# A decoder layer's mixer with its heads ordered by lane group: one or two wide transfers for each factor and coefficient load, operands stored by batch, sums of squares in groups of four

## The chip, the cores and the metric

The kernel runs on one core of a Trainium2 chip. The metric is the device time of one execution in microseconds. Before the change three runs gave a median of 3355.25 us (3353.84 to 3386.32).

## The reference

A pre-norm decoder layer in float32 on x (4 batches, 1024 tokens, 256 channels): a state-space mixer, a cross-attention to 77 context rows, and a mixture of experts, each added to x. The change is in the mixer alone:

```python
bc = jnp.einsum('bti,oi->bto', value, W_bc).reshape(Bsz, Tlen, H, 4, N)
bc = bc / (jnp.sqrt(jnp.sum(bc * bc, axis=-1, keepdims=True)) + EPS)
Bz, Bx, Cz, Cx = (bc[..., 0, :], bc[..., 1, :], bc[..., 2, :], bc[..., 3, :])
def step(carry, inp):
    z, s = carry
    S = 1.0 / (1.0 + dt_t[..., None] * k_t[..., None] + (dt_t * dt_t)[..., None] * A)
    z = S[..., None] * (z - dtE * A[None, :, :, None] * s + dtE * (Bz_t[..., None] * u_t[:, :, None, :]))
    s = s + dtE * z + dtE * (Bx_t[..., None] * u_t[:, :, None, :])
    y = jnp.einsum('bhn,bhnd->bhd', Cz_t, z) + jnp.einsum('bhn,bhnd->bhd', Cx_t, s)
```

There are H = 32 heads of N = 32 states and 16 channels.

## The kernel before

`mixer` works in 16 units `u` of 64 time steps by 4 batches (256 columns, UT). The 32 heads stand in 8 groups `g` of 4 lane groups `j` (32 partitions each); two groups `g` make a pair, so a unit has four pairs `gp` (GP), and `n = 4u + gp` numbers them. Head `g*4 + j` lies in lane group `j`. In `bc`, `fb`, `fc`, `coef` and `pinv` a column is a time step and a batch, `t*4 + b`: the batch is innermost. Each engine has its own program, written out by hand, and they meet at semaphores; SP issues all transfers of the mixer in one program order.

PE: for a later pair, `projected` (four products of 128 x 512, line 605) and `summed` (line 619), which adds the squares of 32 states of a head with the 0/1 matrix `sel`, two of the four vectors at a time. For the pair in hand, `inputs_turned` (line 630), `causal_products` (643), `mixed_states` (663 and 673), `mixed_values` (683), once a unit `outputs` (692). The operands from `bc` are taken with `turns(...)[:, :, b]`, every fourth column.

ACT copies the projected tile to `bc` and squares it into `sq` (one buffer, lines 758 and 761), makes the inverse norms (`norms`), and scales the coefficients (`coefs`).

DVE: `evolve` is the recurrence of a 2 x 2 matrix over 64 steps (lines 918 and 924); `factors(n)` multiplies the inverse norms by step factors (944); `inputs(u,gp)` (957 to 971) and `read_out(u,gp)` (979 to 994) scale and mix the four vectors of a pair; `mask` (1002), `post` (1014 to 1024) and `residual` (1031) follow PE's results. Their order in a unit is in the last loop of DVE's program: `read_out` 0, `post` of the unit before, `inputs` 1, `read_out` 1, `residual`, `inputs` 2, `mask` 0, `read_out` 2, `factors`, `post` 0, `inputs` 3, `mask` 1, `read_out` 3, and then evolve steps of the next unit with the rest between them.

A factor has one value for each head, so it must be spread over 32 partitions. `store_factors(n)` writes `nr` to memory (128 KB), and `load_factors` reads the rows back, each repeated for its lane group: for every `j` and every one of two vectors one transfer of 64 KB, eight in all, into `fb` (vectors 0 and 1) or `fc` (2 and 3). `load_coefs` and `load_ratio` do this with a transfer of 256 KB for each `j`. SP waits for `in_ready` (end of `inputs`) before it refills `fb`, and for `out_ready` (end of `read_out`) before it refills `fc`.

Of the kernel before, what the change touches and what calls it, by code (L numbers as in the profile page):

```python
# [9 lines left out]
ALU = mybir.AluOpType  # L10
# [3 lines left out]
P = 128  # L14
# [4 lines left out]
L = 64  # L19
# [23 lines left out]
def constants():  # L43
# [4 lines left out]
    hn = np.arange(G)[None] * J + jn[:, None]  # L48
# [288 lines left out]
def mixer(nc, d, st, wbc, x, x1):  # L337

    with ExitStack() as ctx:
# [33 lines left out]
        sq = sb("sq", [P, 2, UT])  # L373
# [66 lines left out]

        xv = x.rearrange("(q r u s) m -> u r s q m", q=2, r=2, s=L)
# [148 lines left out]
        def _(pe):  # L590
# [18 lines left out]
            def summed(u, gp, i):  # L609

                n = GP * u + gp
                p = 4 * n + i
                g, first = 2 * gp + i // 2, 2 * (i % 2)
                pe.wait_ge(sq_ready, p + 1)
                if i == 0 and n > 0:
                    pe.wait_ge(nr_root, n)
                for v in range(2):
                    c = first + v
                    mm = pe.matmul(ssp[H * c:H * c + H, 0:UT], sel[:, g, :], sq[:, v, :],  # L619
                                   start=(i < 2), stop=(i >= 2))  # L620
                mm.then_inc(sums_done, 1)

            def inputs_turned(u, gp):
# [4 lines left out]
                for v in range(2):  # L628
                    for b in range(B):
                        mm = pe.transpose(kp[:, v, b * P:(b + 1) * P],  # L630
                                          turns(bc[:, gp, v].rearrange("p i t -> p (i t)"))[:, :, b], ident[:])
                    mm.then_inc(bt_full, 1)

            def causal_products(u, gp):
# [1458 lines left out]
```

## Time and profile before

| | |
|---|---|
| profiled execution, its own time | 3354.0 us |
| its span | 3352.2 us |
| median of three runs | 3355.25 us |
| granted TensorE clock, mean | 0.927 of 2.4 GHz |
| PE busy | 2969.5 us (89%) |
| DVE busy | 2062.2 us (62%) |
| ACT busy | 1303.7 us (39%) |
| DMA queue of SP | 340.20 MB, 36.5% of 16 engines |

The mixer lies between the first projection at 281.8 us and about 2100 us; before it are the input projections, after it the cross-attention and the experts. In a timeline the first number is the start of a piece in us from the span's start, the second its length, and brackets give the idle time of the engine before it with what ended it. A timeline row of SP is the time in which SP issued transfers, not that in which their bytes moved. The DMA share is that of the 16 DMA engines of the core.

### The profile page before, as it was taken

How to read it: one execution, taken by the hardware profiler on the slowest of the kernel's cores; microseconds unless marked ns; L12 is line 12 of the kernel's file. 1: busy time of each engine (PE TensorE's matmuls, PEld its weight loads, DVE VectorE, ACT ScalarE, POOL GpSimd, SP SyncE). 2: the span in 40 equal slices, each digit the busy share in tenths (PEclk: the TensorE clock that was granted, in tenths of full speed). 3: DMA queues.
4: the chain of work that ended last, by engine and by line, in shares of the span. 5: the costliest groups of instructions: out<-in, count | busy, mean ns of one | idle time of the engine just before them, and what ended most of it. 6: DMA issues, size and time to landing. Idle time of an engine off the chain costs nothing. (4 is left out here: it accounts for less than half of the span.)

```text
span 3352.2 us, 84244 instructions
## 1 busy us (share of the span) xinstructions
PE 2969.5 (89%) x34360; PEld 2215.4 (66%) x34360; DVE 2062.2 (62%) x7109; ACT 1303.7 (39%) x2246; POOL 287.1 (9%) x227
## 2 busy tenths in 40 slices
PE   5885799999999999999999998698699389999997
PEld 2344577777787777878778776333376156888886
DVE  5445898989989999999988996455533000111110
ACT  3443345444544455444544552233221011333332
POOL 0000000000000000000000000000002710343433
PEclk9887899999999999999999998799859589999998
DMA  6556332444254324443344322200041211777777
GB/s 226 151 157 172 85 95 64 127 102 97 68 122 115 101 79 97 117 110 88 74 127 102 96 63 69 72 1 1 28 203 60 96 46 35 186 202 202 202 206 216
DMA packets 333204, 373.98 MB, mean 112 GB/s; under 512 B 62254, under 2 KB 294848, under 8 KB 328128
## 3 DMA queue, kind: packets, MB, share of 16 engines
q1 hardware_dynamic: 310400, 340.20, 36.5%
q0 software_dynamic: 22464, 28.95, 4.3%
q8 instruction: 250, 4.10, 0.5%
q14 instruction: 90, 0.74, 0.1%
HBM read 269.17 MB, written 104.04 MB: 111 GB/s over the span
## 5 line engine op out<-in xcount | busy, mean ns | idle before, releaser
L605 PE MATMUL ring<-valt,wbc 128*128 128x256 f32 x4096 | 943.4, 386 | 29.9 <-DMA valt<-valt_scratch 27.6
L605 PEld LDWEIGHTS ring<-valt,wbc 128*128 128x128 f32 x4096 | 772.6, 193 | 166.6 <-issue 61.1
L758 ACT COPY bc<-ring 128x512 f32<-128x512 f32 x256 | 149.6, 584 | 732.4 <-PE ring L605 732.3
L918 DVE TENSOR_TENSOR uu<-phi,coef 128x64 f32<-128x64 f32 x2048 | 359.2, 215 | 2.1
L924 DVE TENSOR_TENSOR phi<-phi,uu 128x64 f32<-128x64 f32 x2048 | 358.9, 215 | 0.0
L2023 DVE TENSOR_SCALAR f_yr<-fp_y,f_meta 128x256 f32<-128x256 f32 x124 | 54.3, 479 | 415.2 <-PE fp_y L1839 415.2
L663 PE MATMUL yp<-bc,hpad 32*32 32x64 f32 x8192 | 260.3, 289 | 3.3 <-DVE hc L1024 2.5
L663 PEld LDWEIGHTS yp<-bc,hpad 32*32 32x32 f32 x8192 | 225.3, 121 | 54.2 <-issue 54.0
L1901 ACT ACTIVATE f_hT<-fp_h,f_b 128x256 f32<-128x256 f32 x248 | 117.6, 474 | 328.2 <-PE fp_h L1830 328.2
L1839 PE MATMUL fp_y<-f_w,f_hT 128*128 128x256 f32 x992 | 230.7, 386 | 7.9
L1712 POOL DMA_INDIRECT acc_scratch<-f_yr,f_meta x124 | 192.6, 1553 | 444.3 <-DVE f_yr L2023 276.4
L1830 PE MATMUL fp_h<-f_xrt,f_w 128*128 128x256 f32 x992 | 227.0, 382 | 0.8 <-ACT f_xrt L1890 0.8
L1699 POOL COPY f_xn<-f_gk 128x32 f32<-128x32 f32 x3 | 0.7, 244 | 2570.7 <-DVE f_rowid L2004 2567.3
L1839 PEld LDWEIGHTS fp_y<-f_w,f_hT 128*128 128x128 f32 x992 | 183.4, 190 | 45.0 <-ACT f_hT L1901 20.7
L1830 PEld LDWEIGHTS fp_h<-f_xrt,f_w 128*128 128x128 f32 x992 | 190.2, 192 | 27.8 <-issue 1.5
L619 PE MATMUL ssp<-sq,sel 128*32 128x256 f32 x1024 | 161.8, 394 | 44.2 <-ACT sq L761 44.1
L1956 DVE TENSOR_TENSOR xres<-fp_y,xres 128x1024 f32<-128x1024 f32 x10 | 12.2, 1224 | 265.5 <-PE fp_y L1767 150.5
L957 DVE TENSOR_TENSOR bc<-bc,fb 128x512 f32<-128x512 f32 x128 | 82.6, 686 | 133.3 <-DMA fb<-fac_scratch 132.8
L1753 PE MATMUL fp_y<-f_ws,f_hT 128*128 128x256 f32 x512 | 126.5, 397 | 42.8 <-issue 42.6
L643 PEld LDWEIGHTS kp<-bc 32*64 32x64 f32 x8192 | 140.5, 203 | 29.0 <-issue 29.0
L761 ACT ACTIVATE sq<-ring 128x512 f32<-128x512 f32 x256 | 153.1, 598 | 5.0 <-PE ssp L619 4.7
L643 PE MATMUL kp<-bc 32*64 32x64 f32 x8192 | 151.9, 306 | 3.3 <-ACT btt L780 2.4
(226 smaller groups left out, 4168.6 us busy)
## 6 DMA issues: line engine op xcount, KB each, us to landing
f_w<-in_W_dram SPq DMA_DIRECT2D x128, 512.0 KB
coef<-par_scratch SPq DMA_DIRECT2D x128, 256.0 KB, 5.8
fb<-fac_scratch SPq DMA_DIRECT2D x512, 64.0 KB, 2.2
fc<-fac_scratch SPq DMA_DIRECT2D x512, 64.0 KB, 2.6
xg_scratch<-f_fill SPq DMA_DIRECT2D x16, 1032.0 KB, 17.1
f_xr<-xg_scratch SPq DMA_DIRECT2D x64, 258.0 KB
vtok_scratch<-p_vtok SPq DMA_DIRECT2D x32, 512.0 KB, 7.1
dub<-vtok_scratch SPq DMA_DIRECT2D x16, 1024.0 KB, 5.5
```

The costliest lines, as they stand in the source:

```text
L605: mm = pe.matmul(ring[:, p % 2, v * UT:(v + 1) * UT], wbc[:, k, g, first + v, :], valt[:, u % 2, k, :], start=(k == 0), stop=(k == 3))
L619: mm = pe.matmul(ssp[H * c:H * c + H, 0:UT], sel[:, g, :], sq[:, v, :], start=(i < 2), stop=(i >= 2))
L643: mm = pe.matmul(kp[L * i:L * i + L, j, b * L:(b + 1) * L], turns(bc[r, gp, v, i, :])[:, :, b], turns(bc[r, gp, 2 + v, i, :])[:, :, b], st ...
L663: pe.matmul(yp[r, b * L:(b + 1) * L], hpad[r, v, i, b, :], turns(bc[r, gp, 2 + v, i, :])[:, :, b], start=(b == 0 and i == 0 and v == 0), s ...
L758: nc.scalar.copy(bc[:, gp, first:first + 2, i // 2, :], o).then_inc(bc_ready, 1)
L761: nc.scalar.activation(sq[:], o, ACT.Square).then_inc(sq_ready, 1)
L918: made[k] = mark(V.tensor_tensor(uu[:, k].rearrange("p i (g b) -> p i g b", b=B), phi[:, t, ::-1, k, :].rearrange("p i (g b) -> p i g b", ...
L924: ins = V.tensor_tensor(phi[:, t + 1, :, k, :], phi[:, t, :, k, :], uu[:, k], ALU.add)
L1712: pool.indirect_dma_start(acc, bass.IndirectOffsetOnAxis(ap=meta[:, par, a, 0:1].bitcast(I32), axis=0), yr[:, par, a, :], None, compute_op ...
L1753: mm = pe.matmul(yp[:, 2 * (nb % 2) + a // 2, (a % 2) * DM:(a % 2 + 1) * DM], hT[:, e, f, a * P:(a + 1) * P], ws2[:, e, f, :], start=(e == ...
L1830: mm = pe.matmul(hp[:, f, 0:RT], w1[:, par, k, f * P:(f + 1) * P], xrt[:, par, k, :], start=(k == 0), stop=(k == 1))
L1839: mm = pe.matmul(yp[:, par, a * DM:(a + 1) * DM], hT[:, par, f, a * P:(a + 1) * P], w2[:, par, f, :], start=(f == 0), stop=(f == 3))
```

## The change

Heads are ordered by lane group: head row `j*8 + g` instead of `g*4 + j`, in the parameters, the biases and `sel`. The rows that a lane group needs then lie side by side in memory. `load_coefs` and `load_ratio` become one transfer of 1 MB, `load_factors` two transfers of 256 KB; `fb` and `fc` change the order of their dimensions to vector, group. The last products of `inputs` and `read_out` are written to `bc` by batch (batch, group, time), and PE reads them in a row; these products now wait for the second of the two products ahead of them, since both write across the same columns. `sq` has two buffers, and `summed` works on four vectors at a time, half as often. In the third pair DVE makes `factors(n0 + 3)` inside `read_out`, ahead of its line 1006.

```diff
-    hn = np.arange(G)[None] * J + jn[:, None]
+    hn = jn[:, None] * G + np.arange(G)[None]
...
+            def all_heads(v):
+                return v.rearrange("(j g) t -> j (g t)", j=J).unsqueeze(1).broadcast_to([J, N, G * UT])
             def load_coefs(u, i):
-                for j in range(J):
-                    sp.dma_start(coef[N * j:N * j + N, i], heads(par(u, 3 * i), j)).then_inc(w_in, 16)
+                sp.dma_start(coef[:, i].rearrange("p g t -> p (g t)"), all_heads(par(u, 3 * i))).then_inc(w_in, 16)
             def load_ratio(u):
-                for j in range(J):
-                    sp.dma_start(pinv[N * j:N * j + N], heads(par(u, 4), j)).then_inc(r_in, 16)
+                sp.dma_start(pinv[:].rearrange("p g t -> p (g t)"), all_heads(par(u, 4))).then_inc(r_in, 16)
...
             def load_factors(dst, signal, n, c0):
                 gp = n % GP
-                src = st["fac"][n].rearrange("(c g i j) t -> g j i c t", c=4, g=GP, i=2)[gp]
-                for j in range(J):
-                    for c in range(2):
-                        sp.dma_start(dst[N * j:N * j + N, :, c, :],
-                                     src[j, :, c0 + c].unsqueeze(0).broadcast_to([N, 2, UT])).then_inc(signal, 16)
+                src = st["fac"][n].rearrange("(c j g i) t -> g c j (i t)", c=4, j=J, g=GP)[gp]
+                for c in range(2):
+                    sp.dma_start(dst[:, c].rearrange("p i t -> p (i t)"),
+                                 src[c0 + c].unsqueeze(1).broadcast_to([J, N, 2 * UT])).then_inc(signal, 16)
...
-            def summed(u, gp, i):
+            def summed(u, gp, half):
...
-                for v in range(2):
-                    c = first + v
-                    mm = pe.matmul(ssp[H * c:H * c + H, 0:UT], sel[:, g, :], sq[:, v, :],
-                                   start=(i < 2), stop=(i >= 2))
+                for i in range(2):
+                    for v in range(2):
+                        c = 2 * i + v
+                        mm = pe.matmul(ssp[H * c:H * c + H, 0:UT], sel[:, g, :], sq[:, i, v, :],
+                                       start=(half == 0), stop=(half == 1))
...
                                 pe.matmul(yp[r, b * L:(b + 1) * L], hpad[r, v, i, b, :],
-                                          turns(bc[r, gp, 2 + v, i, :])[:, :, b],
+                                          flat(gp, 2 + v)[r, b * P + i * L:b * P + (i + 1) * L],
...
                 for i, m in enumerate((m1, m2)):
-                    need(other[i])
-                    V.tensor_tensor(bc[:, gp, 0, i, :], fb[:, i, 1, :], m[:, 1, :], ALU.subtract)
-                    ins = V.tensor_tensor(bc[:, gp, 1, i, :], m[:, 0, :], fb[:, i, 0, :], ALU.subtract)
+                    need(other[1])
+                    V.tensor_tensor(late(flat(gp, 0))[:, i], batches(fb[:, 1, i, :]), batches(m[:, 1, :]), ALU.subtract)
+                    ins = V.tensor_tensor(late(flat(gp, 1))[:, i], batches(m[:, 0, :]), batches(fb[:, 0, i, :]),
+                                          ALU.subtract)
...
+                if between is not None:
+                    factors(between)
                 dve.wait_ge(in_ready, n + 1)
...
-                read_out(u, 2)
-                factors(n0 + 3)
+                read_out(u, 2, n0 + 3)
```

On SP, in the middle of a unit, from the store of factors to the second coefficient row. Before:

```order
L496 DMA fac_scratch<-nr 128x256
L463 DMA coef<-par_scratch 32x8x256 x4
L503 DMA fb<-fac_scratch 32x2x256 x8
L483 DMA sg<-sg_scratch 128x1024
L503 DMA fc<-fac_scratch 32x2x256 x8
L471 DMA pq<-par_scratch 32x256 x3
L473 DMA iqe<-par_scratch 32x8x4 x4
L463 DMA coef<-par_scratch 32x8x256 x4
```

and in the change:

```order
L510 DMA fac_scratch<-nr 128x256
L478 DMA coef<-par_scratch 128x1x2048
L516 DMA fb<-fac_scratch 128x1x512 x2
L497 DMA sg<-sg_scratch 128x1024
L516 DMA fc<-fac_scratch 128x1x512 x2
L485 DMA pq<-par_scratch 32x256 x3
L487 DMA iqe<-par_scratch 32x8x4 x4
L478 DMA coef<-par_scratch 128x1x2048
```

The order is kept; 4 transfers become 1 and 8 become 2, and a destination now begins with 128 partitions.

On DVE, the end of `read_out(0, 2)` (lines 979 to 994 before, 993 to 1010 in the change), `factors` (944, now 957) and the first row of `post` (1014, now 1033). Before:

```order
L985 TENSOR_TENSOR bc<-bc,fc 128x2x256 x2
L988 TENSOR_TENSOR fc<-phi,bc 128x512 x2
L990 TENSOR_TENSOR m<-phi,bc 128x512 x2
L994 TENSOR_TENSOR bc<-fc,m 128x2x256 x2
L944 TENSOR_TENSOR nr<-nr,pq 128x256
L1014 SCALAR_TENSOR_TENSOR m<-valt,skip,yp 128x256
```

and in the change:

```order
L999 TENSOR_TENSOR bc<-bc,fc 128x2x256 x2
L1002 TENSOR_TENSOR fc<-phi,bc 128x2x256 x2
L957 TENSOR_TENSOR nr<-nr,pq 128x256
L1006 TENSOR_TENSOR m<-phi,bc 128x512 x2
L1010 TENSOR_TENSOR bc<-fc,m 128x8x64 x2
L1033 SCALAR_TENSOR_TENSOR m<-valt,skip,yp 128x256
```

The factors stand two pairs earlier, and the last products write 64 columns at a time.

On PE, one pair without `outputs`, from the first products of the later pair (behind `inputs_turned`) to `mixed_values`. Before:

```order
L605 MATMUL ring<-valt,wbc 128x256 x16
L619 MATMUL ssp<-sq,sel 32x256 x2
L643 MATMUL kp<-bc 64x64 x64
L605 MATMUL ring<-valt,wbc 128x256 x8
L619 MATMUL ssp<-sq,sel 32x256 x2
L605 MATMUL ring<-valt,wbc 128x256 x8
L619 MATMUL ssp<-sq,sel 32x256 x2
L663 MATMUL yp<-bc,hpad 32x64 x16
L619 MATMUL ssp<-sq,sel 32x256 x2
L663 MATMUL yp<-bc,hpad 32x64 x48
L673 MATMUL yp<-dub,btt 32x2x16 x32
L683 MATMUL yp<-km,dub 32x64 x16
```

and in the change:

```order
L618 MATMUL ring<-valt,wbc 128x256 x16
L656 MATMUL kp<-bc 64x64 x64
L618 MATMUL ring<-valt,wbc 128x256 x8
L632 MATMUL ssp<-sq,sel 32x256 x4
L618 MATMUL ring<-valt,wbc 128x256 x8
L676 MATMUL yp<-bc,hpad 32x64 x16
L632 MATMUL ssp<-sq,sel 32x256 x4
L676 MATMUL yp<-bc,hpad 32x64 x48
L686 MATMUL yp<-dub,btt 32x2x16 x32
L696 MATMUL yp<-km,dub 32x64 x16
```

The four sums of two are two sums of four; nothing else moves.

## Rows read from the trace of the kernel before

**Rows 1.** Busy time in a stretch, nine units: length, busy us (instructions), clock, DMA share, GB/s.
```profile
480.34:1465.89 985.55, 955.77 (x16147) 774.17 (x16148) 902.63 (x3421) 493.75 (x812) 0.00 (x0) 0.99 0.40 99
```

**Rows 2.** Waits, 480 to 1900 us: us in total, times, longest us.
```profile
DVE bc L957 <- DMA fb<-fac_scratch: 109.2, 26, 8.5
ACT coef L739 <- DMA coef<-par_scratch: 67.7, 13, 8.2
...
PE ssp L619 <- ACT sq L761: 28.2, 10, 5.6
```

**Rows 3.** Timeline of DVE in one unit: start, us, line, instruction, idle before.
```profile
915.50 0.41 DVE L971 TENSOR_TENSOR bc<-m,fb 128x256 f32<-128x256 f32 x1
915.84 0.41 DVE L970 TENSOR_TENSOR bc<-fb,m 128x256 f32<-128x256 f32 x1
...
916.51 1.28 DVE L979 TENSOR_TENSOR fc<-fc,pinv 128x512 f32<-128x512 f32 x2
...
922.71 0.48 DVE L1014 SCALAR_TENSOR_TENSOR m<-valt,skip,yp 128x256 f32<-128x256 f32 x1
923.11 0.41 DVE L1017 TENSOR_TENSOR m<-hc,yp 128x256 f32<-128x256 f32 x1
923.55 0.42 DVE L1018 TENSOR_TENSOR sg<-m,sg 128x256 f32<-128x256 f32 x1
...
931.21 1.28 DVE L979 TENSOR_TENSOR fc<-fc,pinv 128x512 f32<-128x512 f32 x2
...
937.23 0.68 DVE L1031 TENSOR_TENSOR xs<-yp,xs 128x512 f32<-128x512 f32 x1
941.67 1.29 DVE L957 TENSOR_TENSOR bc<-bc,fb 128x512 f32<-128x512 f32 x2 [3.75 <-DMA fb<-fac_scratch]
942.88 1.28 DVE L965 TENSOR_TENSOR fb<-phi,bc 128x512 f32<-128x512 f32 x2
...
953.78 0.41 DVE L944 TENSOR_TENSOR nr<-nr,pq 128x256 f32<-128x256 f32 x1
...
956.08 0.43 DVE L1024 TENSOR_TENSOR hc<-m 128x256 f32<-128x256 f32 x1
961.26 1.29 DVE L957 TENSOR_TENSOR bc<-bc,fb 128x512 f32<-128x512 f32 x2 [4.75 <-DMA fb<-fac_scratch]
```

**Rows 4.** Timeline of SP in the same unit: start, us that issuing took.
```profile
922.48 0.43 SPq L480 DMA_DIRECT2D dub<-vtok_scratch  x1
...
927.65 2.03 SPq L463 DMA_DIRECT2D coef<-par_scratch  x4
932.07 3.59 SPq L503 DMA_DIRECT2D fb<-fac_scratch  x8
...
954.22 0.34 SPq L496 DMA_DIRECT2D fac_scratch<-nr  x1
956.04 3.60 SPq L503 DMA_DIRECT2D fb<-fac_scratch  x8
```

**Rows 5.** Busy time in two short stretches, columns as in rows 1.
```profile
925.00:926.00 1.00, 1.00 (x6) 0.90 (x5) 0.90 (x5) 0.59 (x2) 0.00 (x0) 1.00 0.97 410
926.00:933.00 7.00, 7.00 (x45) 5.75 (x44) 6.97 (x14) 1.55 (x4) 0.00 (x0) 1.00 1.00 271
```

**Rows 6.** Groups of PE instructions, 300 to 2000 us: busy us, mean ns of one.
```profile
L663 PE MATMUL yp<-bc,hpad 32*32 32x64 f32 x7552 | 240.2, 289 | 0.0
...
L683 PE MATMUL yp<-km,dub 128*32 128x64 f32 x1888 | 43.4, 224 | 14.8 <-issue 10.3 <-DVE km L1002 4.4
```

**Rows 7.** Timelines of SP and DVE at the mixer's start.
```profile
302.66 3.78 SPq L463 DMA_DIRECT2D coef<-par_scratch  x8
306.49 6.56 SPq L537 DMA_DIRECT2D par_scratch<-phi  x5
...
320.37 0.21 DVE L903 MEMSET phi<- 128x32 f32 x4 [14.15 <-DMA par_scratch<-phi]
```

More of the change, by code:

```diff
@@ L439, in turns, with batches, flat, late @@
             return v.rearrange("p (t b) -> p t b", b=B)
+        def batches(v):
+            return v.rearrange("p (t b) -> p b t", b=B)
+        def flat(gp, c):
+            return bc[:, gp, c].rearrange("p i t -> p (i t)")
+        def late(v):
+            return v.rearrange("p (b i t) -> p i b t", b=B, i=2)
         xv = x.rearrange("(q r u s) m -> u r s q m", q=2, r=2, s=L)
@@ L607, in projected @@
                 mm.then_inc(ring_full, 1)
-            def summed(u, gp, i):
+            def summed(u, gp, half):
                 n = GP * u + gp
[L612 to L615, printed above, removed]
+                g = 2 * gp + half
+                pe.wait_ge(sq_ready, 4 * n + 2 * half + 2)
+                if half == 0 and n > 0:
                     pe.wait_ge(nr_root, n)
-                for v in range(2):
-                    c = first + v
-                    mm = pe.matmul(ssp[H * c:H * c + H, 0:UT], sel[:, g, :], sq[:, v, :],
-                                   start=(i < 2), stop=(i >= 2))
+                for i in range(2):
[3 more added lines that the diff above has]
+                                       start=(half == 0), stop=(half == 1))
                 mm.then_inc(sums_done, 1)
@@ L630, in inputs_turned @@
                         mm = pe.transpose(kp[:, v, b * P:(b + 1) * P],
-                                          turns(bc[:, gp, v].rearrange("p i t -> p (i t)"))[:, :, b], ident[:])
+                                          flat(gp, v)[:, b * P:(b + 1) * P], ident[:])
                     mm.then_inc(bt_full, 1)
@@ L699, in _ @@
                     projected(0, gp, i)
-                    if gp > 0 or i > 0:
-                        summed(0, gp - (i == 0), (i - 1) % 4)
-            summed(0, GP - 2, 3)
+                    if i == 2:
+                        summed(0, gp, 0)
+                    elif i == 0 and gp > 0:
+                        summed(0, gp - 1, 1)
+            summed(0, GP - 2, 1)
             for u in range(NU):
@@ L758, in projected @@
                 nc.scalar.copy(bc[:, gp, first:first + 2, i // 2, :], o).then_inc(bc_ready, 1)
-                if p > 0:
-                    act.wait_ge(sums_done, p)
-                nc.scalar.activation(sq[:], o, ACT.Square).then_inc(sq_ready, 1)
+                if p >= 2:
+                    act.wait_ge(sums_done, p // 2)
+                nc.scalar.activation(sq[:, p % 2], o, ACT.Square).then_inc(sq_ready, 1)
             def norms(u, gp):
                 n = GP * u + gp
-                act.wait_ge(sums_done, 4 * n + 4)
+                act.wait_ge(sums_done, 2 * n + 2)
                 if n > 0:
@@ L964, in inputs @@
                     need(scaled[i])
[L965 removed]
+                    V.tensor_tensor(split(fb[:, :, i]), rows(1, 0, 2 * gp + i), twice(bc[:, gp, 0, i, :]), ALU.mult)
                 other = [mark(V.tensor_tensor(split(m[:]), rows(0, 1, 2 * gp + i), twice(bc[:, gp, 1, i, :]), ALU.mult))
@@ L992, in read_out @@
                 for i, m in enumerate((m1, m2)):
-                    need(other[i])
-                    ins = V.tensor_tensor(bc[:, gp, 2:4, i, :], fc[:, i], m[:], ALU.add)
+                    need(other[1])
+                    ins = V.tensor_tensor(bc[:, gp, 2:4].rearrange("p c i t -> p c (i t)")
+                                          .rearrange("p c (b i t) -> p i c b t", b=B, i=2)[:, i],
+                                          fc[:, :, i].rearrange("p c (t b) -> p c b t", b=B),
+                                          m[:].rearrange("p c (t b) -> p c b t", b=B), ALU.add)
                 ins.then_inc(out_ready, 1)
@@ L2047, in layouts @@
     w = np.asarray(inputs["L0_attn_W_in"])
-    order = np.concatenate([chan, DI + chan, 2 * DI + 2 * np.arange(H), 2 * DI + 2 * np.arange(H) + 1])
+    rows = (np.arange(G)[None] * J + np.arange(J)[:, None]).reshape(-1)
+    order = np.concatenate([chan, DI + chan, 2 * DI + 2 * rows, 2 * DI + 2 * rows + 1])
     r["W_in"] = w[order].T
@@ L2056, in layouts @@
     r["A_states"] = np.asarray(inputs["L0_attn_A_log"]).reshape(G, J * N).T
-    r["dt_bias_b"] = np.tile(np.asarray(inputs["L0_attn_dt_bias"]), B)[:, None]
+    r["dt_bias_b"] = np.tile(np.asarray(inputs["L0_attn_dt_bias"])[rows], B)[:, None]
     r["ctxT"] = np.asarray(inputs["ctx_768"]).transpose(0, 2, 1)
```

33 lines of the change are left out of this document (15 added, 18 removed).

## The prediction

> **What bounds the kernel now.** I read the page's slices first: the mixer runs from about 280 to 2100 us, and nothing outside it is touched by the change, so the question is the length of its 16 units. The row of busy times over nine whole units (from one load of `dub` to the tenth, 985.55 us) gives 109.5 us a unit, with PE busy 955.8 us and DVE busy 902.6 us [rows 1]. PE is the busier one, yet it is not the one that sets the time. The waits say so [rows 2]: DVE waits for one thing only, `fb`, 109.2 us in 26 waits over the 13 units of that window, 8.4 us a unit; 902.6 us over nine units is 100.3 us of DVE work, and 100.3 + 8.4 = 108.7, nearly the whole unit. PE has waits of its own (28.2 us for `sq` in 13 units), but DVE never waits for PE. So DVE, with the factor loads that it waits for, is the chain; PE runs beside it with 109.5 - 955.8/9 = 3.3 us a unit to spare.
>
> The timeline of DVE in one unit shows the two waits [rows 3]. Let t count from 916.51, when `inputs(u,0)` has ended. `inputs(u,2)` is ready to start at t = 21.4 (the end of the residual) and starts at 25.2; `inputs(u,3)` is ready at 40.0 and starts at 44.75. Before the first, SP issues the 1 MB load of `coef` and behind it the eight loads of `fb` [rows 4]; before the second, DVE makes the factors (t = 37.3), SP stores them, waits 1.8 us for the landing, and issues eight loads for 3.6 us.
>
> **The change, part by part.**
>
> *Issues.* A factor load is 2 transfers instead of 8, a coefficient or ratio load 1 instead of 4. The eight issues take 3.6 us [rows 4], 0.45 each, so two cost 0.9: 2.7 us less between the landing of the store and the last byte of `fb`, if the bytes came at the same speed.
>
> *Bytes.* They don't change: 512 KB for each `fb` or `fc`, 1 MB for each `coef` or ratio, so 7 MB a unit. What changes is how a transfer is cut. Before, both sides of each broadcast begin with 32 partitions (source step 0). Now the destination begins with 128 partitions and the source with the 4 lane groups (`(j g) t -> j (g t)`, then the repeat of 32). No row of this trace shows a transfer whose source begins with fewer than 16 rows, so its speed is bounded from both sides. One end: all 16 DMA engines share it. The other: only as many engines as there are lane groups, 4. The price of an engine: in 925 to 926 us, while the 8 KB rows of `dub` move, the DMA engines carry 410 GB/s at a share of 0.97, so 26.4 GB/s an engine; in the mixed 1 KB traffic of 926 to 933 us 271 GB/s at 1.00, so 17 [rows 5]. I take the end of 4 engines: every broadcast of before offers a multiple of 16 on both sides and fills all engines, and 4 rows offer no equal cut into more than 4. That is a choice, not something a row shows.
> The Trainium skill (DMA: Bandwidth & Descriptors, "Why a DMA increments its semaphore by 16 and not by 1") states that the engine count is the largest number up to 16 that divides the slowest dimension of both patterns, which gives 4 here and speaks against the change; by it the sum below stands, without it the first rival's. No run here shows it yet.
>
> For one engine I take 25 GB/s (2 KB pieces for the factors, 8 KB for the rest, so near the 26.4 and not the 17): 100 GB/s on four. A factor load is then 524/100 = 5.2 us of those four engines, a coefficient or ratio load 10.5 us; a unit needs 8 x 5.2 + 3 x 10.5 = 73 us of them, plus their share of the other transfers. From issue to landing I add 0.6 us ahead and 0.9 behind the data (the store of 128 KB: 1.8 us [rows 4], of which 0.3 is data). All transfers are on one queue, so I let them follow in order.
>
> The unit then goes, in t (data from-to, landing):
> - `fb` for `inputs(u,1)`: 0.7-5.9. `dub` (2.5 us on all engines): 6.6-9.1. `fc`, issued at 6.4 when `read_out(u,0)` ends: 9.1-14.3, lands 15.2; `read_out(u,1)` wants it at 14.7. `valt` and the store to 15.8.
> - `coef` row 0: 15.8-26.3. `fb` for `inputs(u,2)`, issued at 16.6, lies behind it: 26.3-31.5, lands 32.4. Before: 25.2. **+7.2 us.**
> - `sg` to 31.9, `fc` 31.9-37.1 lands 38.0, while `inputs` and `mask` run to 38.5. Hidden.
> - The small loads and `coef` row 1: 37.1-48.2, x store 48.5. The factors are made earlier now, inside `read_out(u,2)`, at 42.5 instead of after it at about 44.9; but the store lies behind `coef` row 1 and lands at 49.6. `fb` for `inputs(u,3)`: issued 49.7, data 50.3-55.5, lands 56.4. Before: 44.75. **+11.6 us** (the 7.2 is in it).
> - `fc` lands 61.6, `read_out(u,3)` wants it at 62.5. The ratio load, issued at about 69, lands by 81; `accumulate` wants its logarithms only 44 evolve steps and three other pieces after the issue. The next factor loads have the 40 us of evolve steps as cover. Hidden.
>
> *DVE.* The last two pairs of `inputs` and the last pair of `read_out` now wait for the second product (`need(other[1])`). Two independent instructions of this size start 0.34 us apart, two with a wait between them 0.44 [rows 3]: 0.1 us at 8 places a unit. Of these 0.6 us adds to the chain. That the last products are read and written by batch costs between nothing (a pair that reads strided rows of `phi` takes 1.28 us as the pair on plain rows does) and, by the instruction of `post` that reads by batch, 0.48 against 0.41 us [rows 3], 0.07 x 24 = 1.7 us a unit; I take nothing, since the first pair is nearer in kind.
>
> *PE.* A matmul of 64 columns that reads every fourth element takes 289 ns, one that reads them in a row 224 [rows 6], so `mixed_states` and `causal_products` should speed up: 65 ns over 4 tiles side by side for 128 instructions is 2 us a group and 8 us a unit in the first alone. The grouping of the sums takes two breaks away in each group. All of it lies beside the DVE chain and is worth nothing while DVE waits longer than now. If the gain did not come, PE's 106 us would still be below the new unit. ACT is held longer by `coef` (5.2 us a unit now [rows 2]; lands 9 us later), which delays PE's second group to about t = 68; `post(u,1)` wants it at 78. Hidden, with 10 us to spare.
>
> *The start.* The two `coef` loads (302.66) are 21 us of four engines instead of a landing at 315; the second parameter store (306.49) is 1.9 MB on all engines and queues behind them: 303.3 + 21 + 5 + 0.9 = 330.2 for the evolve steps, which begin at 320.4 now [rows 7]: +9.8 us.
>
> **Sum.** Units 0 to 14 have coefficient loads: 15 x (11.6 + 0.6) = 183 us; the start 10; the last unit, without coefficients, gives back its two waits, -8. Against the profiled execution's own 3354.0 us (span 3352.2, median of the runs 3355.25, so 1 us off): 3354 + 185 = 3539, rounded to **3540 us**.
>
> **Rivals.**
> *A. All 16 engines carry the wide transfers (faster).* `fb` is then 1.3 us of data. For `inputs(u,2)` it is issued at 16.6 and landed by 19.5, before 21.4: the 3.75 us go. For `inputs(u,3)`: the factors end at 37.7 - 3.8 - 2.4 = 31.5, the store takes 1.8, two issues 0.9, data and latency 2.8: landed at 37.0, wanted at 36.2, so 0.8 us is left of 4.75. The unit is 109.5 - 7.7 + 0.6 = 102.4, which PE (106.2 less 1 to 2 us for the sums, less the contiguous operands) can follow. 16 x -7.1 = -114: 3240 us; near 3290 if PE gains nothing from the contiguous operands (a unit of 105). For it: the shares near 1.00 in every busy stretch [rows 5]. Against: none of those transfers begins with 4 rows. Chance 0.2.
> *B. Four engines, but factor loads are not held behind the coefficient loads (no change).* `fb` for `inputs(u,2)` lands 1.5 + 5.2 us after its issue at 16.6, at 23.3 against 25.2 now. The factors end at 37.7 - 1.9 - 2.4 = 33.4, and the store and `fb` for `inputs(u,3)` take 1.8 + 6.7 from there: 41.9 against 44.75. The unit moves by -2.9 + 0.6: 3354 - 16 x 2.3 + 10 = 3327 us. Against it: all are SP's, on one queue, and the `fb` behind `coef` lands 6.0 us after its last issue now, the one with nothing ahead 1.6 [rows 3, 4]. Chance 0.08.
> *C. Four engines at the 17 GB/s of mixed traffic (much slower).* A factor load is 7.7 us, a coefficient load 15.4. The same list ends with `fb` for `inputs(u,3)` at t = 82: more than 35 us a unit, 3900 us. Against: 17 is what an engine gives while all sixteen compete with 1 KB pieces, which ends with the change. Chance 0.07; part way there (22 GB/s: 6.0 and 11.9 us, the last `fb` at 63) belongs to the forecast and gives 3354 + 15 x 18.6 + 12 = 3645.
>
> **Numbers.** The forecast has 0.65, with a range of its own from 3450 (the waits partly taken up elsewhere, 26.4 GB/s) to 3700 (21 GB/s). The range that holds 8 in 10 must take in part of A: 3235 to 3700. About 1% (34 us) is what can be told from no change: faster 0.2, same 0.08, slower 0.72.
>
> **What would show it.** DVE's wait for `fb` grows from 8 to about 20 us a unit and stays the only one of size, always at `inputs(u,2)` and `inputs(u,3)`; the DMA share in the page hardly moves over 0.3 while `fb` is waited for (four of sixteen engines are 0.25), and stretches of 400 GB/s go; one `coef` takes about 10 us or more from issue to landing; matmuls from `bc` shorten to about 220 ns and PE's idle time grows. Under A the waits for `fb` nearly vanish and PE or DVE work fills the unit. I am wrong if `coef` lands within 5 us of its issue, or if PE, not DVE, turns out to be waited for.

## The result: slower by 11%, and the profile after

The change takes the kernel from 3357.35 us (median of four runs) to 3745.36 us (four runs, 3733.02 to 3755.53): a ratio of 1.113, 95% interval 1.106 to 1.121. The profiled execution took 3751.8 us of its own (span 3750.0), 397.8 more than that of before.

Fourteen whole units, from the second load of `dub` to the last, in the changed kernel. The columns are those of [rows 1].

```profile
516.11:2396.88 1880.77, 1361.06 (x25090) 1117.82 (x25089) 1505.02 (x5322) 754.52 (x1261) 0.00 (x0) 0.87 0.27 81
```

A unit is 1880.77 / 14 = 134.3 us; the same fourteen units were 1535.3 us before, 109.7 each. DVE is busy 107.5 us of a unit, against 100.3 [rows 1]: 7.2 us of new work. PE is busy 97.2 us, 9 less than before, and the DMA share has fallen from 0.40 to 0.27.

The waits of eight of those units (516 to 1592 us), as in [rows 2]: total, times, longest, in us.

```profile
...
ACT coef L752 <- DMA coef<-par_scratch: 206.6, 8, 29.1
DVE bc L970 <- DMA fb<-fac_scratch: 195.3, 16, 13.9
...
PE yp L696 <- DVE km L1021: 126.7, 8, 17.3
...
PE ssp L632 <- ACT sq L774: 81.5, 24, 11.7
ACT pinv L758 <- DMA pinv<-par_scratch: 81.2, 8, 12.8
```

DVE waits 24.4 us a unit for `fb` (8.4 before), still twice a unit, and 1.4 for `fc`, which it never waited for before. 107.5 + 24.4 + 1.4 = 133.3 of 134.3 us: DVE and its waits are the chain as before. ACT waits 26 us a unit for the `coef` rows and 10 for the ratios; PE's waits are for work that DVE and ACT do late.

One unit on DVE, the answer to [rows 3]; t counts from 920.53, the start of `read_out(u,0)`.

```profile
920.53 1.29 DVE L993 TENSOR_TENSOR fc<-fc,pinv 128x512 f32<-128x512 f32 x2
...
925.47 2.11 DVE L1010 TENSOR_TENSOR bc<-fc,m 128x512 f32<-128x512 f32 x2
...
938.74 1.29 DVE L993 TENSOR_TENSOR fc<-fc,pinv 128x512 f32<-128x512 f32 x2 [1.55 <-DMA fc<-fac_scratch]
...
958.07 1.29 DVE L970 TENSOR_TENSOR bc<-bc,fb 128x512 f32<-128x512 f32 x2 [11.73 <-DMA fb<-fac_scratch]
...
961.81 0.61 DVE L983 TENSOR_TENSOR bc<-fb,m 128x256 f32<-128x256 f32 x1
962.33 0.60 DVE L984 TENSOR_TENSOR bc<-m,fb 128x256 f32<-128x256 f32 x1
...
968.63 0.42 DVE L957 TENSOR_TENSOR nr<-nr,pq 128x256 f32<-128x256 f32 x1
...
986.25 1.29 DVE L970 TENSOR_TENSOR bc<-bc,fb 128x512 f32<-128x512 f32 x2 [11.41 <-DMA fb<-fac_scratch]
```

`inputs(u,2)` starts at t = 37.5 and `inputs(u,3)` at 65.7; before they started at 25.2 and 44.75. Over units 2 to 14 of both kernels the means are 38.6 and 66.8 now, 23.8 and 44.4 before. The pair of last products of `read_out` takes 2.11 us.

SP in the same unit, the answer to [rows 4], with ACT's next piece after the ratio load.

```profile
930.97 0.53 SPq L478 DMA_DIRECT2D coef<-par_scratch  x1
940.38 1.07 SPq L516 DMA_DIRECT2D fb<-fac_scratch  x2
941.49 5.89 SPq L497 DMA_DIRECT2D sg<-sg_scratch  x1
...
960.69 0.85 SPq L478 DMA_DIRECT2D coef<-par_scratch  x1
...
969.08 0.34 SPq L510 DMA_DIRECT2D fac_scratch<-nr  x1
976.51 1.16 SPq L516 DMA_DIRECT2D fb<-fac_scratch  x2
...
1000.29 0.55 SPq L481 DMA_DIRECT2D pinv<-par_scratch  x1
```

```profile
1017.81 4.04 ACT L758 ACTIVATE pinv<-pinv,one,amat 128x256 f32<-128x256 f32 x8 [10.32 <-DMA pinv<-par_scratch]
```

The ratio load has no other load of 1 MB beside it and still takes 17.5 us from issue to use. The store of `nr` (969.08) lies behind `coef` row 1, which keeps ACT until 975.50, and lets `fb` be issued 7.4 us later instead of 1.8 [rows 4].

The DMA engines while the ratio rows move (first) and while `fb` and `fc` of the next unit do (second), in the columns of [rows 5].

```profile
1003.00:1016.00 13.00, 11.66 (x208) 9.16 (x206) 12.86 (x84) 2.75 (x5) 0.00 (x0) 1.00 0.28 84
1020.00:1025.00 5.00, 1.18 (x16) 0.37 (x20) 5.00 (x39) 4.98 (x9) 0.00 (x0) 0.50 0.26 100
```

A share of about 0.25 is four engines of sixteen. In these two stretches a busy engine moves 100 / (0.26 x 16) = 24 GB/s of the factors' 2 KB rows and 84 / (0.28 x 16) = 19 GB/s of the ratios' 8 KB rows. That is not a rule of the row length. Four more stretches of the same kernel, each at a share of 0.25 or 0.26: the first coefficient load of all early and late in its course (8 KB rows), `coef` row 1 of the unit above (8 KB), and its `fb` for `inputs(u,3)` (2 KB).

```profile
312.00:314.00 2.00, 2.00 (x11) 1.74 (x11) 0.00 (x0) 0.00 (x0) 0.00 (x0) 1.00 0.26 66
324.00:328.00 4.00, 0.00 (x0) 0.00 (x0) 0.00 (x0) 0.00 (x0) 0.00 (x0) 0.50 0.25 104
971.00:973.00 2.00, 2.00 (x11) 1.77 (x10) 1.91 (x4) 0.00 (x0) 0.00 (x0) 0.96 0.25 102
978.00:982.00 4.00, 2.11 (x130) 1.99 (x131) 0.00 (x0) 4.00 (x10) 0.00 (x0) 0.92 0.26 67
```

So four engines carry between 66 and 104 GB/s (16 to 26 an engine) with rows of 8 KB, and 67 to 100 with rows of 2 KB. What makes the slow stretches slow is not shown by any run.

Groups of DVE and PE instructions, 300 to 2100 us: busy us, mean ns of one.

```profile
L1010 DVE TENSOR_TENSOR bc<-fc,m 128x512 f32<-128x512 f32 x104 | 108.7, 1088 | 1.8
L983 DVE TENSOR_TENSOR bc<-fb,m 128x256 f32<-128x256 f32 x104 | 64.1, 617 | 1.8
L984 DVE TENSOR_TENSOR bc<-m,fb 128x256 f32<-128x256 f32 x104 | 63.6, 612 | 0.0
```

```profile
L676 PE MATMUL yp<-bc,hpad 32*32 32x64 f32 x6436 | 127.3, 234 | 21.9 <-DVE xs L1050 21.9
```

The same groups before, of the same stretch:

```profile
L994 DVE TENSOR_TENSOR bc<-fc,m 128x512 f32<-128x512 f32 x128 | 82.1, 681 | 0.0
L970 DVE TENSOR_TENSOR bc<-fb,m 128x256 f32<-128x256 f32 x128 | 53.2, 416 | 0.0
```

The products by batch cost DVE 16 x 0.20 + 8 x 0.41 = 6.5 us a unit. PE's mean matmul from `bc` fell from 289 ns [rows 6] to 234.

At the start ACT got its `coef` rows at 331.43, and the evolve steps began at 336.46 instead of 320.37 [rows 7].

### The profile page after: what moved, and what is told of

Same layout as the page of the kernel before. It is cut to its first block and busy times, and to the rows that moved or that the text cites. A ratio compares the mean times of both kernels' runs of the same rounds, so it can differ in the third digit from the quotient of the medians.

```text
span 3750.0 us, 83332 instructions
## 1 busy us (share of the span) xinstructions
PE 2827.6 (75%) x34360; PEld 2120.7 (57%) x34360; DVE 2177.4 (58%) x7109; ACT 1290.2 (34%) x2246; POOL 286.7 (8%) x227
## 5 line engine op out<-in xcount | busy, mean ns | idle before, releaser
L618 PE MATMUL ring<-valt,wbc 128*128 128x256 f32 x4096 | 969.0, 394 | 30.2 <-DMA valt<-valt_scratch 28.1
L618 PEld LDWEIGHTS ring<-valt,wbc 128*128 128x128 f32 x4096 | 794.0, 198 | 171.7 <-issue 59.7
L696 PE MATMUL yp<-km,dub 128*32 128x64 f32 x2048 | 54.0, 252 | 260.7 <-DVE km L1021 244.2
L632 PE MATMUL ssp<-sq,sel 128*32 128x256 f32 x1024 | 89.3, 423 | 188.1 <-ACT sq L774 188.1
L676 PEld LDWEIGHTS yp<-bc,hpad 32*32 32x32 f32 x8192 | 145.8, 121 | 88.1 <-issue 88.0
L752 ACT ACTIVATE coef<-coef,nega 128x256 f32<-128x256 f32 x128 | 52.7, 494 | 409.6 <-DMA coef<-par_scratch 409.6
L676 PE MATMUL yp<-bc,hpad 32*32 32x64 f32 x8192 | 167.3, 239 | 34.8 <-DVE xs L1050 27.3
L696 PEld LDWEIGHTS yp<-km,dub 128*32 128x32 f32 x2048 | 41.4, 130 | 262.5 <-DVE km L1021 246.2
L656 PE MATMUL kp<-bc 32*64 32x64 f32 x8192 | 113.1, 253 | 79.3 <-ACT btt L793 74.3
L1974 DVE TENSOR_TENSOR xres<-fp_y,xres 128x1024 f32<-128x1024 f32 x10 | 12.2, 1225 | 270.5 <-PE fp_y L1785 135.6
```

What stands on the lines that cost most here:

```text
L618: mm = pe.matmul(ring[:, p % 2, v * UT:(v + 1) * UT], wbc[:, k, g, first + v, :], valt[:, u % 2, k, :], start=(k == 0), stop=(k == 3))
L656: mm = pe.matmul(kp[L * i:L * i + L, j, b * L:(b + 1) * L], flat(gp, v)[r, b * P + i * L:b * P + (i + 1) * L], flat(gp, 2 + v)[r, b * P + ...
L676: pe.matmul(yp[r, b * L:(b + 1) * L], hpad[r, v, i, b, :], flat(gp, 2 + v)[r, b * P + i * L:b * P + (i + 1) * L], start=(b == 0 and i == 0 ...
L696: mm = pe.matmul(yp[N * j:N * j + N, b * L:(b + 1) * L], dub[:, b, q0:q0 + 2 * DH], km[:, j, b * L:(b + 1) * L], start=False, stop=True, s ...
```

## Experiments

Every ratio is to the kernel before on the same chip (3356.9 to 3362.9 us), with its 95% interval. A unit is the mean over whole units between two loads of `dub`. "Changed kernel" is the one above. For the transfers the question was first what makes a wide load slow (the engines that it gets, against its row length or the number of transfers), and then where that costs time: only where a factor load lies behind a coefficient load (the order), or wherever bytes move (the bytes). For the products it was which side of the stride costs DVE.

### The same loads on all engines, and the products undone

`e1_sixteen`: the changed kernel, each wide load cut by lane group; layout, rows of 8 and 2 KB and products stay.

```diff
+            def one_group(v, j):
+                return v.rearrange("(j g) t -> j (g t)", j=J)[j].unsqueeze(0).broadcast_to([N, G * UT])
...
-                sp.dma_start(coef[:, i].rearrange("p g t -> p (g t)"), all_heads(par(u, 3 * i))).then_inc(w_in, 16)
+                for j in range(J):
+                    sp.dma_start(coef[N * j:N * j + N, i].rearrange("p g t -> p (g t)"),
+                                 one_group(par(u, 3 * i), j)).then_inc(w_in, 16)
```

> The changed kernel, but each wide transfer is cut into one for each lane group: 4 of 32 partitions for a coefficient, ratio or factor load. Bytes, piece sizes (2 KB and 8 KB rows), head order and everything else stay. Theory (spread: a transfer whose source begins with 4 rows is carried by 4 of 16 DMA engines): the loads run on all engines again, a ratio load takes 4 to 6 us from issue to landing instead of 17, DVE's wait for fb falls from 24 us to 1 to 3 us a unit; what stays is the slower last products on DVE, 16 x 0.2 + 8 x 0.41 = 6.5 us a unit; a unit of about 108.5 us, 3335 to 3360 us. Rival (pieces: large repeated rows are slow in themselves, whatever the engines): the waits stay, 3650 to 3745 us. Rival (layout: the operands by batch are the main cost): at least 3650 us as well.

Measured: 3380.49 us, 1.0065 [1.0041, 1.0089]. So the cut of the transfers is 365 us of the 388. It is 20 us above the expected range: a miss in size, while both rivals (3650 us or more) are out.

`e2_plain`: the changed kernel with its wide loads, but products and operands of `bc` in the old layout.

```diff
-                    need(other[1])
-                    V.tensor_tensor(late(flat(gp, 0))[:, i], batches(fb[:, 1, i, :]), batches(m[:, 1, :]), ALU.subtract)
+                    need(other[i])
+                    V.tensor_tensor(bc[:, gp, 0, i, :], fb[:, 1, i, :], m[:, 1, :], ALU.subtract)
```

> The changed kernel, but the last products of inputs and read_out write bc in the old order (batch innermost) and PE takes every fourth column, as before; the wide transfers stay. Theory (spread): only DVE's 6.5 us a unit come back, of which a part turns into longer waits for fb: 3640 to 3690 us, waits for fb 24 to 27 us a unit. Rival (layout is the main cost): 3400 us or less.

Measured: 3701.22 us, 1.1019 [1.0992, 1.1045]. 44 us back, not 55 or more: the products are at 416 and 681 ns again, but the time comes back as waits. Between 500 and 2100 us DVE waits 321.5 us for `fb` and 41.5 for `fc`, where the changed kernel waits 291.2 for `fb`; the unit is 132.1.

The fifth unit of this run on DVE (`read_out(u,0)`, `inputs(u,2)`, `inputs(u,3)`):

```profile
910.20 1.28 DVE L992 TENSOR_TENSOR fc<-fc,pinv 128x512 f32<-128x512 f32 x2
...
947.80 1.29 DVE L970 TENSOR_TENSOR bc<-bc,fb 128x512 f32<-128x512 f32 x2 [13.36 <-DMA fb<-fac_scratch]
...
976.00 1.29 DVE L970 TENSOR_TENSOR bc<-bc,fb 128x512 f32<-128x512 f32 x2 [12.51 <-DMA fb<-fac_scratch]
```

The two starts are at t = 37.6 and 65.8, in the changed kernel at 37.5 and 65.7; the means over units 2 to 14 are 38.6 and 66.9 against 38.6 and 66.8. With the wide loads `inputs(u,3)` starts when its `fb` has come, however long the products ahead of it take. Only those behind it cost time: the eight short ones of `inputs(u,3)` and the next `inputs(u,0)` and the two long ones of `read_out(u,3)`, 8 x 0.20 + 2 x 0.41 = 2.4 us a unit.

`e3_sixteen_plain`: both edits together.

> Both at once: a transfer for each lane group, and the old layout of bc. What stays of the change is the head order with its larger pieces, half the issues of a factor load, sums of four, factors made earlier. Theory (spread plus DVE writes): DVE has 100.3 us of work and about 1 us of waits a unit, PE 106.2 less 2 for the sums: PE binds at 104 to 105 us a unit, 3265 to 3290 us, faster than before by 2%. Rival (pieces): 3630 us. Rival (nothing but the two faults matters): equal to before, 3355 us.

Measured: 3308.18 us, 0.9833 [0.9802, 0.9864], faster than the kernel before. The miss above 3290 is 18 us; the waits that are left are large enough for it (54 us for `fb` between 500 and 2100 us, where about 1 us a unit was expected). Fourteen units of `e1_sixteen` and of `e3_sixteen_plain`:

```profile
474.25:2032.75 1558.50, 1325.02 (x25093) 1087.54 (x25091) 1504.37 (x5323) 758.85 (x1262) 0.00 (x0) 0.94 0.39 98
```

```profile
474.04:1974.32 1500.28, 1443.52 (x25100) 1200.74 (x25101) 1404.96 (x5319) 761.34 (x1264) 0.00 (x0) 0.98 0.41 101
```

With sixteen engines the layout by batch costs DVE 99.4 us over fourteen units and gives PE 118.5 us, and the unit goes from 107.2 to 111.3 us. A gain of 8.5 us a unit on the engine with the larger busy time is lost to 7.1 us on the other. The waits for `fb` in `e1_sixteen` are 35.8 us in those fourteen units, so its unit is nearly DVE's work alone: 107.5 + 2.6 = 110.1 of 111.3.

`e4_scatter`: `e1_sixteen` with the products walked in the order of their sources (time, then batch), so that the reads are in a row and the writes are strided.

```diff
-                    V.tensor_tensor(late(flat(gp, 0))[:, i], batches(fb[:, 1, i, :]), batches(m[:, 1, :]), ALU.subtract)
+                    V.tensor_tensor(late(flat(gp, 0))[:, i].rearrange("p b t -> p t b"), turns(fb[:, 1, i, :]),
+                                    turns(m[:, 1, :]), ALU.subtract)
```

> As the first of these (a transfer for each lane group, operands by batch), but the last products go through their elements in the order of time and batch: they read in a row and write to four places, where the change reads every fourth column and writes in a row. Theory A (DVE pays for reading both operands 16 bytes apart): the 256-element products fall from 617 to about 415 ns and the 512-element one from 1087 to 680; DVE 101 us a unit, PE below 98: 3235 to 3255 us. Theory B (writing out of order costs the same): 600 and 1080 ns, 3335 to 3360 us.

```profile
L1019 DVE TENSOR_TENSOR bc<-fc,m 128x512 f32<-128x512 f32 x128 | 126.0, 1064 | 2.2
L991 DVE TENSOR_TENSOR bc<-fb,m 128x256 f32<-128x256 f32 x128 | 77.7, 607 | 2.2
```

Measured: 3354.27 us, 0.9983 [0.9959, 1.0006]. These groups of DVE show 607 and 1064 ns where reading by batch showed 617 and 1088: the side on which the stride lies hardly matters. One strided side, a write, is enough for nearly the whole price. By the medians this version is 26 us faster than `e1_sixteen`; the slightly shorter products give 16 x 0.010 + 8 x 0.024 = 0.35 us a unit, about 6 us of it, and the rest is not explained (the two profiled executions took 3364.35 and 3365.93 us).

### Which of the loads, and by what

`e5_coef_sixteen`: the changed kernel with only `coef` and `pinv` cut by lane group. `e6_fac_sixteen`: with only `fb` and `fc` cut so.

> The changed kernel with only the coefficient and ratio loads cut by lane group (4 of 32 partitions, rows of 8 KB); the factor loads stay wide. Theory (order: the factors are late because they lie behind 1 MB of coefficients on the same 4 engines): DVE's wait for fb falls from 24 to 5 to 8 us a unit, 3410 to 3460 us. Rival (bytes: each wide byte costs the same, 4 MB of factors and 3 MB of coefficients a unit): 57% of the difference to the version with all loads cut stays, about 3590 us.

> The other half: factor loads cut by lane group, coefficient and ratio loads wide. Theory (order): a factor load now runs on all engines, but its parts on the 4 lowest engines still lie behind the coefficients; waits for fb of 15 to 20 us a unit stay, 3580 to 3650 us. Rival (bytes): about 3535 us.

Measured: 3573.46 us, 1.0616 [1.0559, 1.0673], and 3607.69 us, 1.0732 [1.0674, 1.0789]. The first is far above the 3410 to 3460 us of the idea that only the place behind `coef` matters, and near the 3590 of its rival; the second is inside that idea's range and above the rival's 3535. Over `e1_sixteen` the slow factor loads alone cost 193 us and the slow coefficient and ratio loads alone 227, together 420, and both at once 365. Between 500 and 2100 us the first shows waits of 114.0 us for `fb` in 26 and 82.3 us for `fc` in 26: factor loads are short of time even with a quick load ahead. The second shows 219.1 us for `fb` in 25 waits, up to 13.8 each: the `fb` behind a coefficient load. Both theories are true in part, and their prices nearly add.

`e7_quarters`: the changed kernel, a coefficient or ratio load as four transfers by column, so rows of 2 KB, each still over all four lane groups.

```diff
+                for k in range(4):
+                    sp.dma_start(coef[:, i, 2 * k:2 * k + 2].rearrange("p g t -> p (g t)"),
+                                 all_heads(par(u, 3 * i))[:, :, 2 * UT * k:2 * UT * k + 2 * UT]).then_inc(w_in, 16)
```

> The changed kernel, its coefficient and ratio loads cut by columns: 4 transfers of all 128 partitions, rows of 2 KB instead of 8, so that the source still begins with 4 lane groups. Theory (spread, and rows of 8 KB are slow on 4 engines, since the factor loads with 2 KB rows ran at 100 GB/s and the ratio load at about 65): a ratio load lands 11 to 13 us after its issue instead of 17.5, DVE waits 17 to 20 us a unit, 3640 to 3690 us. Rival (the row's size has nothing to do with it): 17 us and 3745 us. Rival (number of transfers instead of their spread): like all loads cut by lane group, 3380 us.

Measured: 3705.87 us, 1.1015 [1.0958, 1.1072], 16 us above what was expected. Four transfers instead of one, and nearly all of the time stays: neither the number of transfers nor the length of a row is the main matter. The version is about 40 us faster than the changed kernel (the intervals 1.0958 to 1.1072 and 1.106 to 1.121 just touch); in the unit looked at the ratio load takes 15.1 us instead of 17.5, at 95 GB/s and a share of 0.28, 21 GB/s an engine:

```profile
983.00:995.00 12.00, 11.71 (x209) 9.20 (x207) 11.86 (x76) 2.75 (x5) 0.00 (x0) 1.00 0.28 95
```

`e10_pairs`: the changed kernel, a coefficient or ratio load as two transfers of 64 partitions, so that the source of each begins with two lane groups. If each got engines of its own, the two would be done as soon as one with four.

```diff
+                for h in range(2):
+                    sp.dma_start(coef[64 * h:64 * h + 64, i].rearrange("p g t -> p (g t)"),
+                                 all_heads(par(u, 3 * i))[2 * h:2 * h + 2]).then_inc(w_in, 16)
```

> The changed kernel, its coefficient and ratio loads cut into two transfers of 64 partitions, each with a source that begins with 2 lane groups. Theory (spread: the number of rows that the source begins with is the number of engines, and they are always the same first ones): these loads now run on 2 engines, a ratio load takes 27 us or more, DVE waits 20 us a unit longer still: 4000 to 4200 us, slower than the change although the transfers are smaller and more. Rival (a transfer is slow because it is wide, or because there are few of them): faster than the change, 3560 to 3745 us.

Issue of the ratio load, ACT's wait for it, and the engines between:

```profile
993.43 1.11 SPq L484 DMA_DIRECT2D pinv<-par_scratch  x2
```

```profile
1023.51 4.04 ACT L762 ACTIVATE pinv<-pinv,one,amat 128x256 f32<-128x256 f32 x8 [21.13 <-DMA pinv<-par_scratch]
```

```profile
996.00:1022.00 26.00, 13.55 (x217) 10.82 (x215) 25.40 (x167) 3.84 (x7) 0.00 (x0) 0.82 0.15 46
```

Measured: 4178.44 us, 1.2465 [1.2416, 1.2514]. The same bytes now take 30.1 us, at a share of 0.15 (two engines are 0.125) and 46 GB/s. So the count of the first dimension sets the number of engines. The two transfers, issued together, got no more than two between them, so they most likely shared the same two; the trace does not number the engines. This is the run that decides the step of four engines, on which the prediction's direction stood.

### What the rest of the change is worth

`e8_factors_late`: `e3_sixteen_plain` with `factors(n0 + 3)` behind `read_out` again. `e9_sums_of_two`: `e3_sixteen_plain` with one `sq` buffer and sums of two. The cuts are against `e3_sixteen_plain`.

```diff
-                read_out(u, 2, n0 + 3)
+                read_out(u, 2)
+                factors(n0 + 3)
```

```diff
-                pe.wait_ge(sq_ready, 4 * n + 2 * half + 2)
+                pe.wait_ge(sq_ready, p + 1)
...
-                for i in range(2):
-                    for v in range(2):
-                        c = 2 * i + v
-                        mm = pe.matmul(ssp[H * c:H * c + H, 0:UT], sel[:, g, :], sq[:, i, v, :],
-                                       start=(half == 0), stop=(half == 1))
+                for v in range(2):
+                    c = first + v
+                    mm = pe.matmul(ssp[H * c:H * c + H, 0:UT], sel[:, g, :], sq[:, v, :],
+                                   start=(i < 2), stop=(i >= 2))
```

> The version with loads cut by lane group and the old layout of bc (3308 us), with the factors of the fourth pair made after read_out again. If the earlier factors are worth something: DVE's wait for fb at the fourth pair grows by up to 2.4 us a unit, 3325 to 3345 us. If PE binds there: 3308 us.

> The version with loads cut by lane group and the old layout of bc (3308 us), with sq in one buffer and the sums in twos again. If the sums of four carry a part of its gain (each break in the stream of products costs PE about 0.3 us, two breaks fewer in each of 4 groups, so 2 to 3 us a unit of an engine that nearly binds): 3325 to 3350 us. If DVE alone binds: 3308 us.

Measured: 3319.34 us, 0.9864 [0.9808, 0.9919], and 3352.46 us, 0.9979 [0.9956, 1.0002]. The place of the factors is worth about 11 us, with intervals that overlap those of `e3_sixteen_plain`, so no more than a sign. The sums of four with their second `sq` buffer are worth 44 us, 1.5% by the two ratios, and so nearly the whole gain of `e3_sixteen_plain` (1.7%); no run has one of the two without the other. Fourteen units of `e9_sums_of_two`:

```profile
476.34:2011.77 1535.43, 1491.24 (x25089) 1208.05 (x25090) 1407.65 (x5321) 768.04 (x1261) 0.00 (x0) 0.99 0.41 99
```

PE is busy 47.7 us longer than in `e3_sixteen_plain`, the unit is 109.7 instead of 107.2 us, and DVE's own work is the same. The waits of DVE between 474 and 2034 us, `e9_sums_of_two` and then `e3_sixteen_plain`:

```profile
DVE bc L978 <- DMA fb<-fac_scratch: 59.6, 27, 4.8
DVE nr L965 <- ACT nr L793: 32.0, 13, 4.7
```

```profile
DVE bc L978 <- DMA fb<-fac_scratch: 54.0, 25, 3.8
DVE nr L965 <- ACT nr L793: 12.6, 7, 4.8
```

With the factors early and the loads quick, DVE reaches `factors` before the norms are there, and the norms come from PE's sums. These 19 us less of waiting are most of the 35 us between the two stretches; the other 16 are spread over small waits. Two rows of PE's timeline show why the sums are cheaper, four of them in the kernel before and eight in the changed one:

```profile
943.59 0.63 PE L619 MATMUL ssp<-sq,sel 128*32 128x256 f32 x4
```

```profile
940.19 0.64 PE L632 MATMUL ssp<-sq,sel 128*32 128x256 f32 x8
```

Eight sums into four column groups take the time of four into two. Between 300 and 2100 us the sums keep PE busy for 158.7 us in `e9_sums_of_two` and for 81.6 in `e3_sixteen_plain`.

`e11_factors_first`: `e3_sixteen_plain`, the first coefficient row issued behind `fb` of the third pair instead of ahead of it.

```diff
-                    load_coefs(u + 1, 0)
...
+                if more:
+                    load_coefs(u + 1, 0)
```

> The version with loads cut by lane group and the old layout of bc (3308 us), with the first coefficient row issued behind the factors of inputs(u,2) instead of ahead of them. DVE's waits for fb (51.4 us in 13 units there) lose their part at inputs(u,2): if DVE binds, 1 to 3 us a unit, 3265 to 3295 us; if PE binds as well, 3300 to 3308 us.

```profile
DVE fc L1001 <- DMA fc<-fac_scratch: 48.3, 14, 5.1
DVE bc L979 <- DMA fb<-fac_scratch: 39.9, 18, 3.7
```

Measured: 3343.79 us, 0.9949 [0.9921, 0.9977]: a miss. Between 474 and 2034 us `fb` is waited for 14 us less than in `e3_sixteen_plain`, but the 1 MB now lies ahead of `fc`, and DVE waits 48.3 us for that. Of the two places for this megabyte the one of the kernel before is the better.

## Why the prediction was wrong in size and right in direction

**The bound: right.** DVE and its waits for `fb` were named as the chain, and 133.3 of 134.3 us of the new unit are DVE's work and waits. `e1_sixteen` and `e3_sixteen_plain` say the same with other numbers: PE gains 8.5 us a unit and the kernel loses.

**The engines of a wide transfer: right.** The step took the end of four engines, and the shares of 0.26 to 0.28, `e1_sixteen` and `e10_pairs` show it. The rule of the Trainium skill (DMA: Bandwidth & Descriptors, "Why a DMA increments its semaphore by 16 and not by 1") agrees with the runs, four lane groups giving 0.26 and two 0.15. The same section says that such transfers of SP take the lowest-numbered engines; `e10_pairs` agrees as far as it goes, since two transfers of two did not add up to four.

**The order on the queue: right.** `coef` holds up `fb` of `inputs(u,2)`, and `coef` row 1 the store ahead of `fb` of `inputs(u,3)`. Rival B is out: it had the two starts at 23.3 and 41.9.

**The times of the loads on four engines: this step failed.** The list of the unit let `fb` for `inputs(u,3)` land at t = 56.4; `inputs(u,3)` starts at 66.8 in the mean, 10.4 us later. In the unit shown the working and the trace part as follows: `read_out(u,1)` 15.2 and 18.2, `inputs(u,2)` 32.4 and 37.5, the issue of `fb` for `inputs(u,3)` 49.7 and 56.0, its use 56.4 and 65.7. So 3.0 us were lost before `coef` row 0 had its turn (`read_out(u,1)` waits for `fc`, which is issued ahead of it), and another 3.0 between the last issue and its use. The working moved every row at 25 GB/s an engine, from `dub` [rows 5]; measured are 16 to 26, with either length of row, so the size that failed is this one rate and the gaps between loads that it left out. How much of the 10.4 us is slow engines and how much is other transfers on the same engines, no run separates.

`e2_plain` gives the price: with the products at their old cost it took 3701 us, 161 above the forecast of 3540. The loads alone reach the upper edge of the range, which stood for 21 GB/s.

**The last products by batch: this step failed too.** It said between 0 and 1.7 us a unit and took nothing; 6.5 us was measured. The reason given was that a pair on strided rows of `phi` takes no longer. That pair strides between rows and reads each row in order; the new products step 16 bytes from element to element. The row nearer in kind stood beside it, `post` with 0.48 against 0.41 us [rows 3], and even it was used as an end of the range although only one of its operands, a result of PE, is strided. DVE's busy time rose by 7.2 us a unit where the working added 0.6 in all. Behind the wide loads only 2.4 of the 6.5 us lengthen the unit, and the step costs 44 us (3745 against 3701).

The Trainium skill (SBUF — State Buffer, the note on cachelines in the section "Door 1: The DMA port swizzle") states lines of 16 bytes, with a penalty for each access that crosses to a new one, and the prediction did not weigh it. Elements of 4 bytes at a step of 16 never share a line, and the 416 to 617 ns fit that; the note's "for free" up to 4 fp32 does not fit if it means a step of 4 elements, and there the measurement decides.

**The sum.** The unit (134.3) exceeds the 121.7 forecast by 12.6 us: 10.4 up to the start of `inputs(u,3)`, and about 2.3 behind it, the products. (Counted by what DVE does, the same 12.6 are 6.6 us more work and 5.8 more waits, 25.8 against 20.0; but `e2_plain` shows that most of that work only takes the place of waits.) From one profiled execution to the other the 397.8 us lie as follows, with the forecast behind: to the first evolve step 16.1 (9.8); from there to the second load of `dub` 19.7 (12.2); the fourteen units 345.5 (170.8); from the last load of `dub` to the cross-attention's first statistics, 99.5 us against 89.1, 10.4 (-8; 3.5 of the 10.4 only because this load of `dub` is issued earlier in DVE's order than before); after that 6.2 (0), which the change does not touch and nothing here explains. At the start the two `coef` loads moved at 66 GB/s in 312 to 314 us and reached 104 only later. In the last unit DVE's work rose from 56.5 to 66.3 us, and its waits for `fb` fell only from 7.4 to 4.8.

**The range.** Its upper end of 3700 came from a rate of 21 GB/s and nothing for DVE. The loads alone fill it (3701 us, `e2_plain`); with the products it is passed by 45 us. Rival A, all engines, gave 3240 us; `e1_sixteen` is that case, and it came to 3380, mostly because the products were left out. Its other figure, 3290 without PE's gain, has its case in `e3_sixteen_plain`: 3308.

**PE's gain hidden: right.** 289 to 234 ns here, 218 in `e1_sixteen`. But that the grouping of the sums is worth nothing holds only while DVE waits long: with quick loads it was worth 44 us together with the second `sq` buffer, the largest gain in the change.

## What to carry to other kernels

Merging transfers pays by the issue (0.45 us each here) and can cost by the engine: look at the first dimension of both sides, not at the size. Here the source's 4 gave four engines, its 2 gave two, and the transfers that began with 32 partitions on both sides used them all (a share of 1.04 in 979 to 983 us of `e1_sixteen`, while its ratio load moved). A layout is paid by every engine that touches it; before giving the matrix engine its operands in a row, count what the engine that writes them pays for the stride, and which of the two is the one that the end waits for. When a change bundles several edits, try each on the best of the others: here two costly edits hid one worth 1.5%. And price a slower instruction by where it stands: the products ahead of the late `fb` cost nothing here, those behind it their whole length.

## What the runs showed of the hardware

- Elementwise DVE work on 4-byte elements at a 16-byte step: 617 ns for 256 elements against 416 in a row, 1088 against 681 for 512; with only the write strided 607 and 1064.
- Fp32 matmuls of 64 columns whose moving operand lies in a row, 218 ns (`e1_sixteen`), against 289 at a 16-byte step.
- Repeated source rows on four engines: 16 to 26 GB/s an engine with rows of 8 KB (66 GB/s in 312 to 314 us, 104 in 324 to 328, the same two loads) and 16 to 24 with rows of 2 KB (67 in 978 to 982, 100 in 1020 to 1025). The cause stayed open.
- Number of engines by the source's first dimension, as DMA share: 0.26 with 4, 0.15 with 2 (`e10_pairs`).
- An issue on SP can take long when much is queued: one for `sg` 5.89 us behind `coef` and `fb`, where an issue is 0.3 to 0.5 otherwise. It was seen in the changed kernel behind wide loads and not measured by itself.
- Sums of 32 columns: eight in 0.64 us when four column groups are served, four in 0.63 us when two are.
- PE's granted clock was 0.50 (1.2 GHz) in 1020 to 1025 us, while PE waited 9.16 us for `sq`, and 0.87 over the units against 0.99 before. It lengthened PE's work (the projections' matmuls 394 ns against 386), not the chain.
